# Cross attention of a two-layer kernel: keys and values made once in an earlier stage and kept in DRAM, and the attention run by pairs of heads

## The reference

```python
# layer 0, over all 12544 rows
eh = _gelu(_ln(historical_data @ hist_W + hist_b, hist_ln_g, hist_ln_b))
aw = _gelu(eh @ ctx_W1 + ctx_b1) @ ctx_W2 + ctx_b2
aw = jax.nn.softmax(aw, axis=1)
cc = jnp.sum(eh * aw, axis=1)
...
# layer 1 (q = layernorm(x), k = v = ctx_1024)
qp = (q @ Wq.T + bq).reshape(b, l, H, E)
kp = (k @ Wq.T + bq).reshape(b, s, H, E)
vp = (v @ Wq.T + bq).reshape(b, s, H, E)
attn = jax.nn.softmax(scale * jnp.einsum('blhe,bshe->bhls', qp, kp), axis=-1)
out = jnp.einsum('bhls,bshd->blhd', attn, vp)
```

## Time and profile before

| | |
|---|---|
| median of 3 runs | 1225.62 us (1221.63 to 1227.36) |
| time of the profiled execution | 1227.44 us |
| its span in the profile | 1225.6 us |
| PE, PEld, DVE, ACT, POOL busy | 1031.2, 762.3, 713.5, 588.1, 299.4 us |
| HBM read | 44.52 MB |

### The profile page before, as it was taken

The page is one execution under the profiler, slowest core; times in us unless marked ns, Lnnn a source line. Parts: engine busy times, 40 slices in busy tenths (PEclk is TensorE's granted clock), DMA queues, the critical chain, the costliest instruction groups (busy, mean ns, idle before and its releaser), DMA issues. The chain is left out here.

```text
span 1225.6 us, 22100 instructions
## 1 busy us (share of the span) xinstructions
PE 1031.2 (84%) x7674; PEld 762.3 (62%) x7674; DVE 713.5 (58%) x1448; ACT 588.1 (48%) x1192; POOL 299.4 (24%) x401
## 2 busy tenths in 40 slices
PE   4899999999652055865999999999999999999765
PEld 4787777777341032854677777777777777765554
DVE  3556777777656946444866656666566666630131
ACT  2768787787511021211165555655566555664010
POOL 1333333333004301241033224432243322200000
PEclk9999999999866556875599999999999999995566
DMA  2221221120060001163044335433354332450000
GB/s 95 57 64 60 68 64 51 57 64 27 1 257 1 0 21 49 24 128 91 1 106 99 70 92 121 104 95 68 93 120 101 94 75 61 91 154 21 0 1 4
DMA packets 28664, 84.17 MB, mean 69 GB/s; under 512 B 4371, under 2 KB 17652, under 8 KB 27830
## 3 DMA queue, kind: packets, MB, share of 16 engines
q0 software_dynamic: 8512, 38.66, 14.9%
q1 hardware_dynamic: 20086, 44.65, 11.2%
HBM read 44.52 MB, written 0.13 MB: 36 GB/s over the span
## 5 line engine op out<-in xcount | busy, mean ns | idle before, releaser
L1162 ACT ACTIVATE prob<-bank 128x512 f32<-128x512 f32 x392 | 234.1, 597 | 144.2 <-PE bank L846 140.8
L1669 DVE TENSOR_REDUCE unit_max<-bank 128x1 f32<-128x448 f32 x448 | 259.9, 619 | 72.0 <-PE bank L838 70.9
L863 PE MATMUL bank<-prob,vals 128*32 128x128 f32 x3136 | 185.4, 294 | 0.0
L838 PE MATMUL bank<-k_stack,q_base 96*128 96x448 f32 x448 | 179.2, 452 | 0.0
L846 PE MATMUL bank<-q_stack,k_stack 97*128 97x256 f32 x784 | 172.0, 302 | 1.5 <-DMA q_stack<-neg_maxT 1.5
L846 PEld LDWEIGHTS bank<-q_stack,k_stack 97*128 97x128 f32 x784 | 148.0, 199 | 21.9 <-issue 11.5
L548 PE MATMUL bank<-hc_high,w_high 128*128 128x256 f32 x392 | 124.8, 318 | 14.4 <-POOL hc_low L1231 8.4
L548 PE MATMUL bank<-hc_low,w_high 128*128 128x256 f32 x392 | 111.2, 284 | 0.0
L548 PE MATMUL bank<-hc_high,w_low 128*128 128x256 f32 x392 | 111.1, 283 | 0.0
L1388 DVE SCALAR_TENSOR_TENSOR normed<-bank,b_centered,rstd_wide 128x256 f32<-128x256 f32 x196 | 85.5, 478 | 43.8 <-ACT rstd_wide L1049 43.8
L838 PEld LDWEIGHTS bank<-k_stack,q_base 96*128 96x128 f32 x448 | 82.8, 199 | 44.8 <-issue 27.0
(11 more groups left out here) (314 smaller groups left out, 1659.6 us busy)
## 6 DMA issues: line engine op xcount, KB each, us to landing
k_stack<-k_high POOLq DMA_DIRECT2D x112, 224.0 KB, 4.0
hc_raw<-in_ctx_t SPq DMA_DIRECT2D x49, 256.0 KB, 2.8
s_raw<-in_ctx_t SPq DMA_DIRECT2D x14, 896.0 KB, 4.7
k_stack<-k_low POOLq DMA_DIRECT2D x56, 224.0 KB, 3.8
w_ffn<-in_l SPq DMA_DIRECT2D x4, 1920.0 KB, 13.3
w_l<-in_l SPq DMA_DIRECT2D x6, 603.0 KB, 3.9
w<-in_l SPq DMA_DIRECT2D x1, 3012.0 KB
tab<-in_tables SPq DMA_DIRECT2D x1, 1536.0 KB
```

The source lines that it names most:

```text
L838: nc.tensor.matmul(bank[:, bank_of(MAX_BANKS, v), 0:SW], q_base[0:ONE_ROW, g, hh * T:(hh + 1) * T], k_stack[b][0:ONE_ROW, g, w * SW:(w + 1 ...
L863: last = nc.tensor.matmul(bank[at:at + 32, 2 + g % 2, 0:T], vals[:, b, v_at:v_at + 32], prob[:, p % NPB, u % 2, hh * T:(hh + 1) * T], star ...
L1162: A(prob[:, p % NPB, :, :], bank[:, bank_of(EXP_BANKS, p), :].rearrange("p (u t) -> p u t", u=2), ACT.Exp).then_inc(c_exp, 1)
L1669: V.tensor_reduce(unit_max[:, h, w:w + 1], bank[:, bank_of(MAX_BANKS, v), 0:SW], AX_X, ALU.max, negate=True).then_inc(c_red, 1)
```

## The change

Keys and values of all 12544 rows are made in the history stage, from the parts of the context that are there already, and written to DRAM; the context is not read again. `keys_product(n)` adds 12 matmuls of 256 columns to chunk n on PE, into bank 7; ACT adds the bias and copies out (`keys_full`, 2 operations of 256 elements); PE turns the result (`values_turn`, 4 transposes of 128 columns) into the same bank 7; ACT copies that as values (`values_copy`, 512 elements); DVE splits the keys (`keys_parts`, a cast and a subtraction of 512 elements). SP stores both parts of the keys after every chunk (2 DMAs of 256 KB) and the values after every fourth (1.1 MB in runs of 544 bytes). `mean_square` moves to bank 4, which frees bank 7.

The context stage now goes by the eight pairs of heads instead of by blocks. For a pair, SP loads the keys of all 12544 rows in 7 pieces of 1792 rows, 6 DMAs each, 4.8 MB for a pair, and the values in one DMA of 1.7 MB; both have two buffers. `maximum_group` makes the maxima: for 448 rows two matmuls, one for each head, on partitions 0 to 48 and on 64 to 111, into two banks, and one DVE maximum over 896 elements. There are 28 such units for a pair. With the maxima of the whole pair known before its scores begin, nothing is rescaled; the pair's sums stay in one bank. The maxima of pair s+1 are made during the exponentials of pair s, those of pair 0 in front. The loop is a list of 131 steps (`step_plan`): three exponentials (6 score matmuls, 256 columns, now in three banks), the 12 fp32 matmuls that weigh the three of the step before, and in 96 of the 131 steps one group (two units, 4 matmuls of 448 columns). Seven times a pair's maxima are turned (`turn_maxima`) and copied to `q_stack` by ACT (`maxima_row`) instead of by a DMA.

Gone are: the reading of the context in the context stage, `context_high`, `context_low`, `keys_high`, `keys_low`, `stack` with its 168 DMAs, `value_tile`, `value_copy`, `new_maxima`, `rescale`, `add_sums`, and in layer 0 the keys of two blocks, two fills of 7168 elements with ones (`k_stack0`, `k_stack1`) and the fill of `vals` on POOL.

```diff
-SC = 896
-NJ = S // SC
...
-MAX_BANKS, EXP_BANKS = (0, 1, 6), (4, 5)
+TILES = S // P
+MU = 448
+UNITS = S // MU
+EU = TILES // 2
...
+STEP = 3
+LEAD = 2
+NPB = 12
...
+MAX_SLOTS, EXP_BANKS, SUM_BANK = (0, 2), (4, 5, 6), 7
...
+            def store_keys(n):
+
+                sp.wait_ge(c_kl, n + 1)
+                cols = slice(n * CH, (n + 1) * CH)
+                sp.dma_start(k_out[0, :, :, cols], k_high[:, n % 2].bitcast(F32)).then_inc(k_stored[n % 2], 16)
+                sp.dma_start(k_out[1, :, :, cols], k_low[:, n % 2].bitcast(F32)).then_inc(k_stored[n % 2], 16)
...
+            def load_keys(s, c):
+
+                cols = slice(c * CHUNK, (c + 1) * CHUNK)
+                if s >= 2:
+                    sp.wait_ge(c_sc, exp_at[EU * (s - 2) + CHUNK_EXPS * (c + 1) - 1][0] + 1)
...
+            def keys_product(n):
+                b = n % 2
+                wait_at(pe, c_vc, n)
+                for m in range(KD):
+                    cols = slice(m * P, (m + 1) * P)
+                    last = product(bank[:, 7, m * CH:(m + 1) * CH],
+                                   [(w[:, k, cols], v[:, b, k]) for k in range(KD)
+                                    for w, v in ((x_high, hc_high), (x_low, hc_high), (x_high, hc_low))])
+                last.then_inc(c_kp, 1)
+
+            def values_turn(n):
+                pe.wait_ge(c_kf, n + 1)
...
                 if 1 <= n <= NCH:
                     mean_square(n - 1)
+                    values_turn(n - 1)
                 if n < NCH:
                     project(n, 1)
...
+                if n < NCH:
+                    keys_product(n)
...
+            def maximum_group(g):
+
+                s = g // (UNITS // 2)
+                for u in (2 * g % UNITS, 2 * g % UNITS + 1):
+                    n, at = max_ring.take()
+                    wait_at(pe, c_red, max_ring.free(n))
...
+                    for hh, rows in ((0, slice(0, 3 * HD + 1)), (1, slice(64, 64 + 3 * HD))):
+                        last = nc.tensor.matmul(bank[:, at + hh, 0:MU], q_max[rows, s, :], k_stack[s % 2][rows, cols],
+                                                start=True, stop=True)
+                    last.then_inc(c_max, 1)
...
+            for exps, turns, groups in step_plan():
+                for e in exps:
+                    scores(e)
+                done_now = []
+                for e in waiting:
+                    if done_now and e % EU == 0:
+                        break
+                    weigh(e)
+                    done_now.append(e)
+                waiting = waiting[len(done_now):] + list(exps)
+                for s in turns:
+                    turn_maxima(s)
+                for g in groups:
+                    maximum_group(g)
...
+            def keys_full(n):
+                act.wait_ge(c_kp, n + 1)
+                wait_at(act, c_vt, n - 1)
+                wait_at(act, c_kl, n - 1)
+                for m in range(KD):
+                    ins = A(k_full[:, n % 2, m, :], bank[:, 7, m * CH:(m + 1) * CH], ACT.Identity, bias=xb[:, m:m + 1])
+                ins.then_inc(c_kf, 1)
...
+            def keys_parts(n):
+                b = n % 2
+                dve.wait_ge(c_kf, n + 1)
+                wait_at(dve, k_stored[b], 32 * (n // 2))
+                V.tensor_copy(k_high[:, b], k_full[:, b]).then_inc(c_kh, 1)
+                dve.wait_ge(c_kh, n + 1)
+                V.tensor_tensor(k_low[:, b], k_full[:, b], k_high[:, b].bitcast(F32), ALU.subtract).then_inc(c_kl, 1)
...
                 if 0 <= n - 1 < NCH:
+                    keys_parts(n - 1)
                     variance(n - 1)
...
+            done(V.tensor_copy(by_pair(q_max[:, :, :]), stacked), "q_max")
             for hh in range(2):
...
+            def reduce_unit(s, u):
+
+                n, at = max_ring.take()
+                dve.wait_ge(c_max, n + 1)
+                if u == 0:
+                    wait_at(dve, c_hm, s - 1)
+                V.tensor_reduce(unit_max[:, s % 2, u, :], bank[:, at:at + 2, 0:MU], AX_X, ALU.max,
+                                negate=True).then_inc(c_red, 1)
```

More of the change, by code:

```diff
@@ new lines, in _ @@
+            dve_s.wait(sp, "x1")
+            sp.wait_ge(c_ones, 16)
+            fill(0)
+            for c in range(CHUNKS):
+                load_keys(0, c)
+            dve_s.wait(sp, "x3")
+            load_values(0)
+            fill(1)
+            for c in range(CHUNKS):
+                load_keys(1, c)
+            load_values(1)
+            for s in range(2, NG):
+                for c in range(CHUNKS):
+                    load_keys(s, c)
+                load_values(s)
+            sp.wait_ge(c_sc, exp_at[EU * (NG - 1) - 1][0] + 1)
@@ new lines, in turn_maxima, with scores @@
+            def turn_maxima(s):
+                n, at = turn_at[s]
+                pe.wait_ge(c_hm, s + 1)
+                wait_at(pe, c_exp, exp_ring.free(n))
+                for hh in range(2):
+                    last = nc.tensor.matmul(bank[MAX_ROW:MAX_ROW + 32, at, hh * T:(hh + 1) * T],
+                                            neg_max[:, hh, :].bitcast(F32), ident, start=True, stop=True)
+                last.then_inc(c_sc, 1)
+            def scores(e):
+                s, u = divmod(e, EU)
+                n, at = exp_at[e]
+                if u == 0:
+                    pe.wait_ge(c_exp, turn_at[s][0] + 1)
+                wait_at(pe, c_exp, exp_ring.free(n))
+                for t in range(2):
+                    k = 2 * u + t
+                    last = nc.tensor.matmul(bank[:, at, t * 2 * T:(t + 1) * 2 * T],
+                                            k_stack[s % 2][0:STACK, k * P:(k + 1) * P], q_stack[0:STACK, s, :],
@@ L933, in _ @@
+            for e in waiting:
+                weigh(e)
+            pe.wait_ge(c_red, NG * UNITS)
+            for g in range(NG):
+                pe.wait_ge(c_ev, g + 1)
+                last = nc.tensor.transpose(bank[:, g // 4, (g % 4) * P:(g % 4 + 1) * P], o_part[:, g, :], ident)
+            last.then_inc(c_ot, 1)
             dve_s.wait(pe, "o1")
@@ L1192, in _, with maxima_row @@
-            for k in range(KT):
-                value_copy(0, 0, k)
-            context_slot(0, 0, first=True)
-            context_slot(0, 1)
-            with act.Fori(1, NJ // 2 - 1) as i:
-                for b in range(2):
-                    context_slot(i, b)
-            context_slot(NJ // 2 - 1, 0, build=False)
-            context_slot(NJ // 2 - 1, 1, build=False, more=False)
-            sums_copy(NJ - 1, NG - 1)
+            def maxima_row(s):
+                n, at = turn_at[s]
+                act.wait_ge(c_sc, n + 1)
+                if s == 0:
+                    dve_s.wait(act, "q_stack")
+                A(q_stack[MAX_ROW:MAX_ROW + 1, s, :], bank[MAX_ROW:MAX_ROW + 1, at, 0:2 * T],
+                  ACT.Copy).then_inc(c_exp, 1)
@@ L1204, in _ @@
+            for exps, turns, groups in step_plan():
+                for e in exps:
+                    exponentials(e)
+                if ready is not None:
+                    sums_copy(ready)
+                    ready = None
+                for s in turns:
+                    maxima_row(s)
+                for e in exps:
+                    if e % EU == EU - 1:
+                        ready = e // EU
+            sums_copy(NG - 1)
             pe_s.wait(act, "ff5")
```

669 lines of the change are left out of this document (230 added, 439 removed).

## The result

The changed kernel takes 1049.36 us (median of 4 runs, 1046.74 to 1051.34) where the kernel before, run on the same chip, takes 1223.82 us: a ratio of 0.857, 95% interval 0.854 to 0.860. The forecast of 1066 us was 1.6% too high. The profiled execution took 1046.74 us, with a span of 1044.7.

The account below looks back on a forecast made before the run. PE was taken to set the pace in the history and context stages. From 1225.6 us: history +98, layer 0 -36.4, ahead of the loop +9.5, loop -232, end +1, giving 1066 us; range 1024 to 1145, the forecast's own 1035 to 1095.

Parts of the forecast that it names:

- the price of 2.0 us a chunk: History stage: added matmuls, transposes and an allowance for ScalarE cost PE 2.0 us in each chunk.
- the multiplication by 49: History stage: the 2.0 us a chunk is paid in full in all 49 chunks, +98 us.
- The allowance of 0.2 us a chunk for ScalarE's group exponential: History stage: estimated 0.2 us a chunk because ACT also has the group's exponential in one chunk of eight.
- the second rival: History stage: PE waits for ACT on bank 7 in every chunk, +71, 1137 us; chance 0.14.
- Layer 0, -43 for -36: Layer 0: removed key matmuls, waits, fills and collisions, and a shorter way to the first maximum, save 36.4 us.
- the collision with the fill of `vals`: Layer 0: POOL's fill lengthened a 256-element DVE operation; with the same effect of `s_low`, -6.6 us.
- the other collision: Layer 0: POOL's `s_low` made a 256-element DVE operation take 3.97 us instead of 0.43; part of -6.6 us.
- Ahead of the loop, +9.6 for +9.5: Before the loop: pair 0's maxima need 30 DVE reductions first, 32.4 us in place of 22.9, +9.5.
- The loop, -236 for -232: Context loop: 96 steps of 2.35 us, 35 of 1.70, turns and clock start, 300 us in all, -232.
- side by side: Context loop: the two heads' maxima matmuls overlap on row halves, 0.38 us, a step of 2.21 us, loop 287 us.
- The rival of 1089 us: Context loop: the heads' maxima run one after the other, or half rows cost more; loop 23 us longer; chance 0.20.
- a loop at 1.2 GHz: Rival, context loop: TensorE keeps the low clock, +37 instead of -232, 1335 us, or 1263 side by side; chance 0.05.

Follow-up runs that it names:

- keys_early: Changed kernel, but in history chunks with a group's exponential ScalarE copies the keys between the two deferred feature pairs, not behind them: 1036.25 us.
- same_rows: Changed kernel, but both heads' maxima made on rows 0 to 48 of the array, not on two row halves: 1085.91 us.
- half_reduce: Changed kernel, but each VectorE maximum reads only half the columns, 448 elements in place of 896: 1026.67 us.
- gap7: Changed kernel plus 16 VectorE copies of 256 elements ahead of the last pair's maxima, so TensorE idles once: 1056.90 us.
- b_light: Kernel before, with TensorE's keys and values in the loop cut to one small matmul each: median 1210.12 us, profiled execution 1134.41 us.
- act_q: Changed kernel, but ScalarE makes q_stack right after q_max, ahead of maxima_row(0), and VectorE makes only q_max: 1048.16 us.

## Why the prediction was right, and where it was not

**Right in its chain.** Each stage moved in the direction of its term, but for the last (-1 for +1), and the largest came out within 2% of its size: the loop at 298 us where the text had 300, a chunk near 8.0 us, 32.5 us ahead of the loop where it had 32.4, steps without maxima at 1.70. The span is 21 us shorter than the sum: 8 in the history, 7 in layer 0, 4 in the loop, 2 at the end.

**History, +90 for +98.** In the window from 50 to 300 us the kernel after has 251 rows of `hc_high,w_high`, 31.4 chunks, 7.97 us each; the price of 2.0 us a chunk was right. The step that failed is the multiplication by 49. In the first 60 us the kernel before waited 5.9 us for `normed` ahead of these matmuls, and the kernel after did not: there the added work filled waits that existed. The allowance of 0.2 us a chunk for ScalarE's group exponential was about right in sum (12.3 / 49 = 0.25), and of the kind the second rival named, but it is six bigger waits and not a toll on each chunk; keys_early took it away.

**Layer 0, -43 for -36.** The mixture gave 14.0 for 11. The sum had only the matmuls of the keys and the wait for `s_low`; I held the rest to be dense, and it was not quite. The stretch behind it gave 22.5; the terms that belong there (5.4 and 12.4, and 3.1 for the collision with the fill of `vals`) make 20.9. Ahead of the mixture the sum had the other collision, 3.5 us, and 1 for the fill that was mostly hidden (it starts at 462.4 us), and 6.9 went; VectorE's casts of the weights (0.43 and 0.69 us) had stood there too and were in no term, and where the other 1.3 us came from stays open. The mechanism of the collision is shown.

**Ahead of the loop, +9.6 for +9.5.** The reductions are the bound: 28 in 28.03 us.

**The loop, -236 for -232.** The number was right in part by luck, since two errors met. I took the maxima to lie between "side by side" and "one after the other", as no row showed half rows, and came to 2.35 us a step; the mean of the timeline's 2.30 and 2.46 is 2.38. In fact they run wholly side by side (same_rows), and the rest is the change of shape, 0.23 to 0.25 us and not 0.14 (half_reduce), with less than 0.1 us of waiting between the two engines. So the term of the maxima with their change was mis-sized in both its parts. The rule of the Trainium skill that the prediction weighed (TensorEngine Tiling (Array Packing), Tiling Modes: row tiles of 64 rows work in parallel) was thus right as to the halves, and its 2.21 us were short only by the change and the waiting. The rival of 1089 us, "one head after the other", is what same_rows built, and it came out at 1086.

**The clock.** I gave 0.05 to a loop at 1.2 GHz and argued with the array's share of a step. The forecast held: 0.99. But STEP 1 shows how near the rival is: with one exponential between two changes the loop takes 628 us, and the whole kernel 1381, slower than before. What the change gains in the loop (236 us) is then 86 us of moved work, paid for by 90 in the history, and 150 us that are left over and go to the new order of work. They are a remainder and were not measured as one: of its parts the runs show the row halves against the same rows (31 us) and three exponentials between changes instead of two (about 30 us); what two instead of one are worth, no run prices apart from the clock. That the clock was up in the last pair as well, worth 22 us in my price, is part of this; I had left it within the range without a reason for either side. The reason that the prediction gave for the low clock in the last slots, a wait that had cut in and a loop that stayed there, fits gap7 and b_light.

**Open.** That the clock rises some 6 us into the loop in one trace, 11 in another and 15 in same_rows was read from traces and not tried by itself. A loop of single exponentials kept the full clock for the last 33 us of b_light; whether it would over a whole loop was not tried. b_light's own clock rose 38 us into its loop, with single exponentials and, between some of them, turns and maxima, so one exponential between changes does not forbid the rise in every mixture of work.

## What to carry to other kernels

Price a change of array shape as an item of its own, count the changes, and batch the same kind of work between them up to the number of free PSUM banks; with too few at a time this loop never got its full clock, and that and the changes together cost four times what the changes alone were to cost (332 us for 86). Work moved to another stage is seldom free, so judge the move and the reordering that it permits apart. Where a helper engine's work is long once in eight rounds, look at what waits behind it in its queue: the keys' copy put ahead of two of four deferred operations was worth 13 us.

## What the runs showed of the hardware

- Two matmuls on row halves of the array (rows 0 to 48 and 64 to 111, 448 columns) overlap wholly: four take 0.62 us from start to start, and 1.02 us on the same rows.
- TensorE can be busy in 99% of the time (621 of 627 us) and be granted 0.50 throughout, in a loop that starts at 0.50 and has one exponential between changes of shape (STEP 1); with two between changes it was 1.00 from 10 us on (STEP 2). Single exponentials that had the full clock kept it: 1.00 over the last 33 us of b_light's loop.
- After an idle time of 5.6 us in a dense loop the clock was down for one step, 3.9 us from the turn of the maxima to full speed, and the whole gap cost 7.5 us.
- A VectorE operation of 256 elements beside a GpSimd operation of 1792 lasts as long as that one does: 3.18 us for 0.41.
- 2.0 us won ahead of the loop stood against 2.3 us lost in it, where the clock rose some 11 us into the loop and not 6 (act_q).
